# Turning 128x128 blocks on TensorE: one transpose, or four 64x64 products with an identity

## The reference, cut to what matters

```
qkv = shift_token(x) @ wqkv                       # 256 -> 3 x 512
q, k = rotary_xpos(l2norm(q) * qs, l2norm(k) * ks) # 8 heads of 64
sim  = q k^T * 8, masked to a window of 128 rows
attn = softmax(sim); out = attn v
x = x + out @ wo
h = layernorm(shift_token(x)) * g + b
x = x + (a * gelu(g)) @ w2 + b2,  a, g = split(h @ w1 + b1)
```

## Time and profile before

| | before |
|---|---|
| median of 3 runs | 1365.91 us (1365.69 to 1367.13) |
| the profiled execution, its own time | 1370.5 us |
| its span (first to last instruction) | 1368.5 us |
| mean granted TensorE clock | 0.999 of full |
| busy: PE, PEld | 98%, 90% |
| busy: DVE, ACT, POOL | 76%, 69%, 58% |

### The profile page before, as it was taken

How to read it: one execution, slowest core, us unless ns; L and a number is a source line. 1 busy time by engine, 2 the same in 40 slices (tenths; PEclk the granted TensorE clock), 3 DMA queues, 4 the chain that set the end, 5 groups by cost and what they waited for, 6 DMA issues and landing times.

```text
span 1368.5 us, 32692 instructions
## 1 busy us (share of the span) xinstructions
PE 1340.9 (98%) x11503; PEld 1232.9 (90%) x11503; DVE 1033.6 (76%) x3003; ACT 939.0 (69%) x2662; POOL 798.3 (58%) x640
## 2 busy tenths in 40 slices
PE   8999999999999999999999999999999999999997
PEld 7999898779999999999999998899999999999987
DVE  5777765678777777777777878877777777777774
ACT  6887776577666666666666777766666666666672
POOL 1221221566666666666666767866666666666653
PEclk9999999999999999999999999999999999999999
DMA  5323112100111111100001211111111111111101
GB/s 178 104 93 109 61 48 102 56 20 31 31 31 31 31 30 29 29 29 29 29 30 31 73 31 39 39 39 39 38 38 38 37 37 37 37 37 38 31 31 33
DMA packets 50517, 63.41 MB, mean 46 GB/s; under 512 B 8403, under 2 KB 32105, under 8 KB 50409
## 3 DMA queue, kind: packets, MB, share of 16 engines
q1 hardware_dynamic: 50408, 61.99, 14.6%
HBM read 38.17 MB, written 16.78 MB: 40 GB/s over the span
## 4 chain that ended last, share of the span: by engine, by line
PE 77%; ACT 8%; DVE 7%; POOL 4%; issue 2%; DMA 2%; SPq 0%; POOLq 0%; DVEq 0%
PE pb L571 37%; PE pb L909 8%; PE pb L840 6%; PE pb L923 6%; PE pb L857 6%; PE pb L872 4%; PE pb L947 4%; ACT x_p L1112 4%; PE pb L884 2%; ACT x_pt L1118 2%; POOL n_inv L1843 1%; DMA x_in<-x 1%; PE pb L796 1%; PE pb L585 1%; POOL r_cos L1855 1%
## 5 line engine op out<-in xcount | busy, mean ns | idle before, releaser
L1251 ACT ACTIVATE p_t<-p_t,s_nm 128x128 f32<-128x128 f32 (+1 forms) x512 | 226.1, 446 | 11.8 <-DVE s_nm L1619 9.4
L571 PE MATMUL pb<-h_hi,w_hi 128*128 128x256 f32 x704 | 209.3, 297 | 1.5 <-DVE h_lo L1583 1.2
L1843 POOL TENSOR_TENSOR n_inv<-n_cl,half_neg 128x16 f32<-128x16 f32 x64 | 205.7, 3213 | 5.3
L571 PE MATMUL pb<-h_hi,w_lo 128*128 128x256 f32 x704 | 198.4, 282 | 0.0
L571 PE MATMUL pb<-h_lo,w_hi 128*128 128x256 f32 x704 | 198.4, 282 | 0.0
L1879 POOL TENSOR_TENSOR hg_lo<-hg,hg_hi 128x256 fp32r<-128x256 f32 (+1 forms) x192 | 143.2, 754 | 67.6 <-DVE hg_hi L1650 67.6
L1848 POOL TENSOR_TENSOR r_cos<-r_cos,r_sin 128x1024 f32<-128x1024 f32 x64 | 158.0, 2469 | 14.3 <-DVE r_sin L1606 13.5
L571 PE MATMUL pb<-wqkv_hi,xt_hi 128*128 128x512 f32 x384 | 162.8, 424 | 0.2 <-DVE xt_lo L1374 0.2
L1619 DVE CUSTOM_DVE_ANT_0 p_t<-pb,mask_t 128x128 f32<-128x128 f32 (+1 forms) x512 | 149.2, 352 | 17.1 <-PE pb L840 16.9
L1643 DVE SCALAR_TENSOR_TENSOR hg<-pb,b_t,gl 128x256 f32<-128x256 f32 (+1 forms) x192 | 91.7, 478 | 87.8 <-ACT gl L1234 65.4
L571 PE MATMUL pb<-wqkv_lo,xt_hi 128*128 128x512 f32 x384 | 152.1, 396 | 0.0
(11 more groups left out here) (147 smaller groups left out, 3961.9 us busy)
## 6 DMA issues: line engine op xcount, KB each, us to landing
y_state<-x SPq DMA_DIRECT2D x32, 256.0 KB, 2.0
x_cur<-y_state SPq DMA_DIRECT2D x32, 256.0 KB, 2.6
x_res<-y_state SPq DMA_DIRECT2D x32, 256.0 KB, 2.8
x_in<-x SPq DMA_DIRECT2D x16, 256.0 KB, 2.9
x_state<-x SPq DMA_DIRECT2D x16, 256.0 KB, 2.0
x_orig<-x_state SPq DMA_DIRECT2D x16, 256.0 KB, 2.9
out<-x SPq DMA_DIRECT2D x16, 256.0 KB, 2.2
x<-x SPq DMA_DIRECT2D x32, 112.0 KB, 2.3
```

The lines of the kernel that those rows point to most:

```text
L571: mm = pe.matmul(dst, s, m, start=(n == 0 and k == 0), stop=(n == len(pairs) - 1 and k == 2))
L1251: e = nc.scalar.activation(pu, pu, ACT.Exp, bias=s_nm[:, j, k:k + 1], scale=-1.0, accum_out=s_sum[:, j, k:k + 1])
L1843: nc.gpsimd.tensor_tensor(n_inv[:, t], n_cl[:, t], half_neg[:], ALU.pow).then_inc(pool_inv, 1)
```

## The change

1. `quarter_turn` is new: a 128x128 block is turned as four plain fp32 products, each with a 64x64 piece of the block as weights and a 64x64 identity moving. The two pieces of a row half go to two column halves of one bank's partitions, and the two row halves go to two neighbouring banks.
2. `turn_qk` uses it for all 16 blocks, in two steps of 8 blocks over two banks each instead of four steps of one bank; the first step waits for what steps 0 and 1 waited for, the second for the outcome of `out_lo` and of `residual`.
3. Units 2 and 3 of the probabilities (8 of 24 blocks) are turned in pairs by `turn_p_two`, with one wait for both; the other four units keep `pe.transpose`.
4. `scores` issues each product twice, once for queries 0 to 63 and once for 64 to 127 (weights of 64x64).
5. ScalarE's copies of these read two banks at once (`probs_copy_two`, `copy_qk`); their number and size stay the same.
6. All bank numbers go through a table `PHYS`, so that the pairs of banks are neighbours. For the very first item, the bank of the first 128 rows of keys is looked up twice and the rotation of those keys reads the bank of the queries: those values differ from the reference's, the amount of work does not.

```
+        PHYS = [0, 1, 2, 3, 7, 4, 6, 5]
-        PT_BANK = [5, 7, 5, 7, 4, 7]
-        QT_BANK = [5, 3, 7, 2]
+        PT_BANK = {0: 5, 1: 7, 4: 4, 5: 7}
+        PT_BANKS = slice(4, 6)
+        QT_BANKS = [slice(3, 5), slice(5, 7)]
...
+            def quarter_turn(banks, col, source):
+
+                for row in range(2):
+                    for c in range(2):
+                        mm = pe.matmul(pb[c * DH:c * DH + DH, (banks.start, banks.stop - 1)[row], col:col + DH],
+                                       source(slice(row * DH, row * DH + DH), c * DH),
+                                       ones_at[row * DH:row * DH + DH, row * DH:row * DH + DH],
+                                       start=True, stop=True)
+                return mm
...
+                pe.sem_inc(scores_go, 1)
                 for k in range(heads):
                     for u in (2 * j, 2 * j + 1):
                         h = heads_of(u)[k]
                         ch, r = h // 2, (h % 2) * DH
-                        mm = pe.matmul(pb[:, S_BANK[u], k * keys:k * keys + keys], qk_t[r:r + DH, 0, ch, q_cols],
-                                       qk_t[r:r + DH, 1, ch, 0:keys], start=True, stop=True)
+                        for rows in (slice(0, DH), slice(DH, P)):
+                            mm = pe.matmul(pb[rows, PHYS[S_BANK[u]], k * keys:k * keys + keys],
+                                           qk_t[r:r + DH, 0, ch, q_cols.start + rows.start:q_cols.start + rows.stop],
+                                           qk_t[r:r + DH, 1, ch, 0:keys], start=True, stop=True)
...
+            def turn_p_two(a, b, d, u):
+
+                pe.wait_ge(dve_pn, at(b, UNITS, u + 2))
...
+                elif u == 2:
+                    pe.wait_ge(act_pt, at(b, UNITS, 2))
...
+                for i in range(2):
+                    for k in range(4):
+                        mm = quarter_turn(PT_BANKS, (4 * i + k) * DH,
+                                          lambda rows, c: p_t[rows, u + i, k * P + c:k * P + c + DH])
+                    mm.then_inc(pe_pt, 1)
...
-            def turn_qk(a, b, c, k):
-                if k == 0:
+            def turn_qk(a, b, c, half):
+                if half == 0:
                     pe.wait_ge(pool_qk, at(a, NT, NT))
                     if b is not None:
-                        pe.wait_ge(act_pt, at(b, UNITS, 3))
-                elif k == 1 and has_next(a):
-                    pe.wait_ge(act_xhi, at(plus(a, 1), 1, 1))
-                    pe.wait_ge(dve_xlo, at(plus(a, 1), 1, 1))
-                elif k == 2 and b is not None:
-                    pe.wait_ge(dve_olo, at(b, 2, 2))
-                elif k == 3 and c is not None:
-                    pe.wait_ge(dve_hg, at(c, FC, 4))
-                for j in range(2):
+                        pe.wait_ge(act_pt, at(b, UNITS, UNITS))
+                    if has_next(a):
+                        pe.wait_ge(act_xhi, at(plus(a, 1), 1, 1))
+                        pe.wait_ge(dve_xlo, at(plus(a, 1), 1, 1))
+                else:
+                    if b is not None:
+                        pe.wait_ge(dve_olo, at(b, 2, 2))
+                        pe.wait_ge(dve_x1, at(b, 1, 1))
+                pe.sem_inc(quarters_go, 1)
+                for j in range(4):
                     for t in range(NT):
-                        col = (2 * k + j) * P
-                        mm = pe.transpose(pb[:, QT_BANK[k], j * T + t * P:j * T + t * P + P],
-                                          r_cos[:, t, col:col + P], id_f)
+                        mm = quarter_turn(QT_BANKS[half], (j * NT + t) * DH,
+                                          lambda rows, c: r_cos[rows, t, (4 * half + j) * P + c:(4 * half + j) * P + c + DH])
                 mm.then_inc(pe_qkt, 1)
...
             def copy_qk(a, k):
-                act.wait_ge(pe_qkt, at(a, 4, k + 1))
+                act.wait_ge(pe_qkt, at(a, 2, k // 2 + 1))
```

More of the change, by code:

```diff
@@ L577, in idle_products @@
                 for _ in range(n):
-                    pe.transpose(pb[:, b, 0:P], id_f, id_f)
+                    pe.transpose(pb[:, PHYS[b], 0:P], id_f, id_f)
+            def quarter_turn(banks, col, source):
[6 more added lines that the diff above has]
+                return mm
             def turn_x(n):
@@ L622, in x_probs @@
                 for k in range(4):
-                    mm = pe.transpose(pb[0:CTX, u % 2, k * P:k * P + P], x_p[:, u, k, :], id_f)
+                    mm = pe.transpose(pb[0:CTX, PHYS[u % 2], k * P:k * P + P], x_p[:, u, k, :], id_f)
                 mm.then_inc(x_ptr, 1)
@@ L853, in turn_p @@
                     pe.wait_ge(act_v, at(a, NT, NT))
[L854 to L855 removed]
+                elif u == 5:
+                    pe.wait_ge(act_pt, at(b, UNITS, 4))
                 for k in range(4):
[L857 removed]
+                    mm = pe.transpose(pb[:, PHYS[PT_BANK[u]], k * P:k * P + P], p_t[:, u, k * P:k * P + P], id_f)
                 mm.then_inc(pe_pt, 1)
+            def turn_p_two(a, b, d, u):
+                pe.wait_ge(dve_pn, at(b, UNITS, u + 2))
+                if u == 0:
+                    pe.wait_ge(dve_max, at(b, UNITS, 5))
+                    if d is not None:
+                        pe.wait_ge(dve_x2, at(d, 1, 1))
+                elif u == 2:
+                    pe.wait_ge(act_pt, at(b, UNITS, 2))
+                else:
+                    pe.wait_ge(act_pt, at(b, UNITS, 4))
+                pe.sem_inc(quarters_go, 1)
[4 more added lines that the diff above has]
+                    mm.then_inc(pe_pt, 1)
             def weigh_late(a, b, c, par, half):
@@ L981, in run_l @@
                     hidden(a, b, c, 0)
-                    turn_p(a, b, d, 2)
-                    turn_p(a, b, d, 3)
+                    turn_p_two(a, b, d, 2)
                     hidden(a, b, c, 1)
@@ L1054, in run_l @@
                     turn_qk(a, b, c, 0)
-                    turn_qk(a, b, c, 1)
                 if c is not None:
@@ L1058, in run_l @@
                 if a is not None:
-                    turn_qk(a, b, c, 2)
-                    turn_qk(a, b, c, 3)
+                    turn_qk(a, b, c, 1)
             def between(g):
@@ L1596, in rotate @@
                 half = DH // 2
-                first = qkv_bank(a, t, 0)
-                qk = pb[:, first:first + 2].rearrange("p j (h d) -> p j h d", d=DH)
+                first, second = PHYS[qkv_bank(a, t, 0)], PHYS[qkv_bank(a, t, 1)]
+                qk = [pb[:, first].rearrange("p (h d) -> p h d", d=DH), pb[:, PHYS[second]].rearrange("p (h d) -> p h d", d=DH)]
                 for j in range(2):
                     nc.vector.tensor_tensor(r_cos[:, t, j * INNER:j * INNER + INNER].rearrange("p (h d) -> p h d", d=DH),
-                                            qk[:, j], cos_t[:, ly, t, j].unsqueeze(1).broadcast_to([P, HEADS, DH]), ALU.mult)
+                                            qk[j], cos_t[:, ly, t, j].unsqueeze(1).broadcast_to([P, HEADS, DH]), ALU.mult)
                 for s in range(2):
                     o = r_sin[:, t].rearrange("p (j h d) -> p j h d", j=2, d=DH)[:, :, :, s * half:s * half + half]
-                    i = qk[:, :, :, half - s * half:DH - s * half]
                     w = sin_t[:, ly, t, :, s * half:s * half + half].unsqueeze(2).broadcast_to([P, 2, HEADS, half])
-                    e = nc.vector.tensor_tensor(o, i, w, ALU.mult)
+                    if second == first + 1:
+                        i = pb[:, first:first + 2].rearrange("p j (h d) -> p j h d", d=DH)
+                        e = nc.vector.tensor_tensor(o, i[:, :, :, half - s * half:DH - s * half], w, ALU.mult)
+                    else:
+                        for j in range(2):
+                            e = nc.vector.tensor_tensor(o[:, j], qk[j][:, :, half - s * half:DH - s * half], w[:, j], ALU.mult)
                 e.then_inc(dve_rope, 1)
@@ L1642, in gate @@
                     dve.wait_ge(pool_hglo, at(plus(c, -1), FC, FC))
-                nc.vector.scalar_tensor_tensor(out=hg[0:rows, m], in0=pb[0:rows, W1_BANK[m], 0:T],
+                nc.vector.scalar_tensor_tensor(out=hg[0:rows, m], in0=pb[0:rows, PHYS[W1_BANK[m]], 0:T],
                                                scalar=b1_t[0:rows, ly, 0, m:m + 1], in1=gl[0:rows, m % 3],
```

101 lines of the change are left out of this document (54 added, 47 removed).

## The result

The changed kernel takes 1439.08 us (median of 4 runs, 1438.42 to 1439.84) against 1365.80 (4 runs, 1365.37 to 1367.13): a ratio of 1.0535, 95% interval 1.0517 to 1.0553. It is 73 us slower where 34 were forecast. 1439 lies inside the stated range, but the range reached there for another reason.

What follows compares the result with a forecast made beforehand. TensorE's own product stream was taken to bound the kernel; 0.99 us for blocks plus 0.12 for turns less 0.05 for scores, 1.06 us an item times 32, added 34 us to 1365.9, giving 1400 us, range 1386 to 1480.

Steps and rivals of the forecast that it cites:

- the price of an item: One loop item on TensorE: 0.99 us for tile blocks plus 0.12 for turns less 0.05 for scores, 1.06 us more.
- Issued twice: Quarters of queries, keys and probabilities: each plain fp32 product is issued twice, giving 192 trace rows an item.
- Four together: Quarter turns: four 64x64 tiles run together, 0.115 us a turn against 0.11 for a transpose, 0.12 us more an item.
- In and out: Edges of the three quarter blocks an item: entering and leaving the tiles costs 0.33 us each, 0.99 us an item.
- Scores -0.05: Scores by halves: products take the same time, only the first load shrinks, gaining 0.05 us an item.
- Nothing waits for the copies: Scores behind turn_qk's copies: copies end later but 0.3 us remains, so the scores do not wait; cost nothing.
- The floor of about 25 ns between starts: Small products: the skill's rule would give 0.2 us a turn and about 1466 us; the prediction trusted the trace instead.
- Times 32: 34 us: Whole run: the 1.06 us of one item multiplied by 32 items, 34 us more.
- All this I cost at nothing: turn_qk's later copies and new waits, with ScalarE's and DVE's amounts unchanged: no added time.
- PE busy throughout: Sign expected in the changed loop: an iteration of 35.2 us with TensorE busy for all of it.
- quarters that overlap less: Rival at the quarter turns: fewer than four tiles overlap, 0.13 to 0.22 us a turn, 1414 to 1480 us; chance 0.18.

Runs made afterwards that it cites:

- the split block: Changed kernel with TensorE's loop written out, plus one full-width transpose in the middle of both blocks of queries and keys: 1426.48 us, ratio 1.0435.
- Experiment 1: Changed kernel with TensorE's loop over the items written out, other engines keeping their loops: 1403.04 us, ratio 1.0262; the kernel before written out likewise: 1367.30 us.
- 4: Kernel before with four unused semaphore increments behind each split product in TensorE's loops, body about 2031: 2041.62 us with the loop, 1990.16 us written out.
- 5: Changed kernel without probability quarters: with two thirds of score halves 1420.36 us, loops at slot 0 1409.59 us; without score halves, loops at slot 192, 1435.64 us.
- the body of 1665: Changed kernel with only queries and keys in quarters, no probability quarters or score halves: 1395.07 us as built, 1435.64 us with its loops placed at slot 192.
- 1437: Changed kernel with only units 2 and 3 of the probabilities in quarters, queries, keys and scores as before: 1380.33 us, ratio 1.0096.
- 1735: Changed kernel without probability quarters and with only two thirds of the scores by halves: 1420.36 us as built, 1409.59 us with loops placed at slot 0.
- the hint: Changed kernel, loops kept, with one more instruction at the head of TensorE's loop announcing the target of the jump back: 1427.82 us, ratio 1.0450.

## Why the prediction was right and wrong

**Right, but for a small error of size: the price of an item.** Issued twice: 192 rows an item. Four together: 0.117 us a turn where I took 0.115; the starts of the 64 products of a block lie 15 ns apart on the mean, and they come in fours, three steps of 7 ns and one of some 38. In and out: 0.30 us by the split block; a whole block 1.32 us, where 0.92 + 0.33 = 1.25 was forecast, which leaves it 0.38, and why it is more than in the split block is open. Scores -0.05. By parts, the block of probabilities costs 0.37 as forecast, and the two of queries and keys 0.83 where 2 x (0.33 + 0.04) = 0.74 was forecast: that is the 0.08 or so that the item is off. Nothing waits for the copies, and the row of waits for qk_t stands at 1.7 us after 1.3 in the earlier trace rows. The sum, 1.06 against 1.14, is off by 32 x 0.08 = 3 us, and the written-out kernel, 1403.04, is 3 us from the predicted 1400.

The floor of about 25 ns between starts, which the prediction cites from the Trainium skill (TensorE: Matmul & The Clock Gate, "Wait — 56ns, not 53.3ns?") and turns down, is contradicted here too: 192 starts at 15 ns are 2.9 us an item, and at 25 ns they would have been 4.8.

**Wrong: the sum times 32.** The step that failed is "Times 32: 34 us", which takes every item for one like the item that was priced. ("All this I cost at nothing" is not it: that was said of the copies and of the new waits, and they do cost nothing. What failed had no term at all.) I cut out one iteration before and took the changed program to be the same iteration with other products. I counted that the quarters are issued twice and priced the time of these instructions, but not the place they take: TensorE's body grew from 1215 to 2021, from at most six blocks to at least eight, and "PE busy throughout" was false six times. The missing term is six jumps of 3.85 us and 2.1 us of lowered clock behind each, 35.6 us. Experiment 1 removes it whole, 4 makes one without a quarter, and 5 switches it on and off by the place of the loop alone.

**The range.** It reached to 1480 for quarters that overlap less. That rival is false, and that 1439 fell inside is no merit of the argument.

The Trainium skill (Runtime: NRT & Kernel Launch, Instruction fetch mechanics) has the mechanism: instructions are fetched in blocks of 16 KiB, and a taken branch to a block outside the window of two that is held at a time waits for the fetch of that block. The trace agrees on the fetch, with 16 KB a packet and some 4 us a jump. It does not agree on the window of two: the loop of before, 1215 instructions in at least five blocks, jumps back with the instruction queue silent. The same section gives TensorE 2048 instructions, which is eight blocks; by that the body of 1665 laid in eight would not stall, and it stalls for 4.5 to 4.8 us at every jump. The runs put the limit at seven blocks, 1792.

## What to carry to other kernels

When an edit adds instructions to a hardware loop, count the loop's body per engine as well as its time: here bodies of 1215 to 1437 cost nothing that shows at a jump, 1665 and 1735 in seven blocks of 256 cost 0.3 us, and eight blocks or more cost some 4 us plus a lowered clock. Before trusting "price of an iteration times their number", look at the instruction queue inside the loop: silence means that the body fits, and a program beyond the limit can be written out or its loop placed anew (here at 4.3 and 2.1 us where the two loops are entered). Turns in quarters are at best as fast as transposes here (0.117 us against 0.11), and each trip into the tiles and out costs 0.3 to 0.4 us besides, so they do not pay at any length of a block. Halves paid only in the scores, which were tiled already, and there by 0.05 us an item.

## What the runs showed of the hardware that was not expected

- The jump's price is a step: 0.3 us with seven blocks, 4.5 to 4.8 us with eight, for the same 1665 instructions. In eight blocks the whole body is fetched anew for each jump, 26 packets for three jumps against 2.
- At every jump that stalls, TensorE resumes 1.7 to 2.0 us after a packet of instructions has landed.
- A loop beyond the limit moves more instruction packets than the same program written out (157 against 143).
- A stall of 4 us costs 6 on the mean of the six: the granted clock goes to 0.50 and is at 1.00 again 7 to 10 us after the stall began. With the hint, stalls of 1.4 to 1.9 us left it at 1.00.
- A semaphore increment on TensorE between its products is not free: 0.096 us each, with what the lowered clock (0.870) takes.
- Written out, TensorE can run short of instructions where small products stand close: with 128 issued products of 15 ns in a block the supply broke off 19 times, for 10.8 us in all.
